# Similarity stage of a graph network: the owners' scans write PSUM in six runs, and each run is multiplied from there

## The chip, the cores and the metric

The kernel runs on one core of a Trainium2 chip. The metric is the device time of one launch in microseconds (us). Three runs of the kernel before took 16588.64, 16588.69 and 16592.46 us, median 16588.69.

## The reference

Four graph layers run over 12,500 nodes with 64 features each and 212,500 directed edges, sorted by `dst`. After each layer comes a residual sum and a layer norm. The changed stage is in the third layer:

```python
Wh = h @ W + b
row, col = (edge_index[0], edge_index[1])          # src, dst
dot = jnp.sum(Wh[row] * Wh[col], axis=-1)
nr, nc = norms of Wh[row] and Wh[col]
sim = dot / jnp.maximum(nr * nc, EPS)
base = adj_v * sc * no_diag
prop_pos = segment_sum((base * relu(sim))[:, None] * Wc, row)
prop_neg = segment_sum((base * -relu(-sim))[:, None] * Wc, row)
return scale * (coeff[0] * prop_pos + coeff[1] * prop_neg + coeff[2] * Wh)
```

## The kernel before

The kernel is a sequence of phases with a barrier between any two. Edges are padded to 128 x 1664: partition p holds 1664 consecutive edges, and an edge pass goes over them in 26 chunks of 64 edges per partition (NCH = 26, T = 64). The third layer's edges stand in the order of their row node (`src`), so the edges of one owner are neighbours.

`similarity_pass` (line 2270) is one such pass. For each chunk it needs two rows of 65 numbers for each edge, the 64 features of Wh and its norm:

- The other end's row is gathered. `gathers` (line 919) issues 64 indirect DMAs for a chunk from GpSimd (POOL), each of which fetches one row for each of 128 partitions from `tab65`, into `rows[b]`, one of two buffers. GpSimd may refill a buffer once the messages of the chunk that used it are made (semaphore `msg`), and once the chunk's indices are there.
- The owner's row is not gathered. An earlier phase wrote it into `spread` at the owner's first edge only, with zeros elsewhere. SyncE loads a chunk of it as `own` (line 2312), ScalarE turns it to feature-major order in `UB` (line 2351), 65 features of 65 places each, where place 0 carries the value from the chunk before. VectorE then spreads it over the owner's edges with a scan, state = mask * state + x (line 2401). `mask` lies in PSUM and is 0 at an owner's first edge, and at place 0 of each feature, so that one scan can run over several features.

In a chunk VectorE works in one written order: the first half of an unrelated side job (`dist.dve`, line 1046, the distance values of the fourth layer, 16 edges per partition of it beside each chunk); three scans over 22, 22 and 21 features, in place in `UB` (line 2401); the carry copy of place T to place 0 (line 2404); then, once the gathered rows have landed, the product `tmp = u * g` over 64 edges x 64 features (line 2416), its sum over features (line 2417), the product of the norms (line 2418) and seven small instructions that turn the two into a weight `a`; the message `MB = g * a` (line 2429); three scans that sum messages by owner (line 2434); a carry copy; and the second half of the side job. ScalarE copies the sums back to edge order in `tmp` (line 2363), and SyncE stores them (line 2319). ScalarE refills `UB` once the messages are made, and the mask once the message scans are done.

SyncE's order in a step is: wait until the chunk before's rows have landed (for the index buffer), load indices, base weights, `own` and the side job's input, then wait for ScalarE's copy and store it. `gains`, `ss` and `a` (two names in the tile `small`) lie in PSUM too.

Of the kernel before, what the change touches and what calls it, by code (L numbers as in the profile page):

```python
# [8 lines left out]
ALU = mybir.AluOpType  # L9
# [3 lines left out]
P = 128  # L13
F = 64
# [5 lines left out]
T = 64  # L20
# [13 lines left out]
def gnn_resnorm(nc, x_in, src_0, dst_0, attr3_0, attr64_0, attr64T_0, w_0, w2_0, W, out):  # L34
# [11 lines left out]
    def ps(ctx, name, shape, dt=F32):  # L46
        unique[0] += 1
        return ctx.enter_context(nc.psum_tensor(f"{name}_{unique[0]}", shape, dt))
# [3 lines left out]
    def sem(name):  # L52

        unique[0] += 1
        phase_sems.append(nc.alloc_semaphore(name=f"{name}_{unique[0]}"))
        return phase_sems[-1]
# [72 lines left out]
    DW = 16  # L129
# [2140 lines left out]
    def similarity_pass(last):  # L2270


        W_, TB, FM = F + 1, T + 1, 22
        runs = lambda w: [(f, min(f + FM, w)) for f in range(0, w, FM)]
        S = lambda n: [sem(f"L2_{n}{b}") for b in range(2)]
        q = lambda n: sem(f"L2_{n}")
        idx_in, rows_in, base_in_ = S("idx"), S("rows"), S("base")
# [3 lines left out]
        with ExitStack() as c, nc.Block() as block:  # L2281
            idx = [alloc(c, f"idx{b}", [P, T], I32) for b in range(2)]
            rows = [alloc(c, f"rows{b}", [P, T, W_]) for b in range(2)]
            own = alloc(c, "own", [P, T, W_])
            base = [alloc(c, f"base{b}", [P, T]) for b in range(2)]
            tmp = alloc(c, "tmp", [P, T, F])
            UB, MB = alloc(c, "UB", [P, W_, TB]), alloc(c, "MB", [P, F, TB])
            dot, nn, b2 = (alloc(c, f"s{n}", [P, T]) for n in range(3))
            mask, pa, gains = ps(c, "mask", [P, FM, TB]), ps(c, "pa", [P, P]), ps(c, "gains", [P, 4, F])
            small = ps(c, "small", [P, DW + T])  # L2290
            ss, a = small[:, 0:DW], small[:, DW:DW + T]
            UB_flat, MB_flat, mask_flat = (t.rearrange("p f t -> p (f t)") for t in (UB, MB, mask))
            by_edge = lambda t: t.rearrange("p f t -> p t f")
            dist = Distances(c, "L2", 3, 1, pa, gains, ss)

# [49 lines left out]
            def _(act):  # L2345
                def take(ch):
                    act.wait_ge(own_in, ch * 16 + 16)
                    if not (isinstance(ch, int) and ch == 0):
                        act.wait_ge(msg, ch)
                    act.wait_ge(own_kept, ch + 1)  # L2350
                    act.activation(UB[:, :, 1:TB], own.rearrange("p t f -> p f t"), ACT.Copy).then_inc(taken, 1)

                def flags(ch):
# [30 lines left out]
            def _(dve):  # L2384
# [2 lines left out]
                dve.memset(mask[:, :, 0:1], 0.0).then_inc(begun, 1)  # L2387
                dve.memset(last[:, :], 0.0).then_inc(begun, 1)
                dist.start(dve)
                NS = 10  # L2390

                def step(i, b):
                    ch = i * 2 + b
# [1 line left out]
                    dist.dve(dve, i, b, 0, 0)  # L2395
                    dve.wait_ge(taken, ch + 1)
                    dve.wait_ge(masked, ch + 1)
                    dve.wait_ge(own_kept, ch + 1)
                    for f0, f1 in runs(W_):
                        x = UB_flat[:, f0 * TB:f1 * TB]  # L2400
                        t = dve.tensor_tensor_scan(x, mask_flat[:, 0:(f1 - f0) * TB], x, 0.0, ALU.mult, ALU.add)
                    t.then_inc(filled, 1)
                    dve.wait_ge(filled, ch + 1)
                    dve.tensor_copy(UB[:, :, 0], UB[:, :, T]).then_inc(own_kept, 1)
                    u, g = by_edge(UB[:, :, 1:TB]), rows[b]
                    dve.wait_ge(rows_in[b], (i + 1) * 16 * T)
                    dve.wait_ge(base_in_[b], (i + 1) * 16)
                    if not first:
                        dve.wait_ge(stored, ch * 16)
                    n = [0]  # L2410

                    def link(ins):
                        n[0] += 1
                        ins.then_inc(steps, 1)
                        dve.wait_ge(steps, ch * NS + n[0])
                    link(dve.tensor_tensor(tmp[:, :, :], u[:, :, 0:F], g[:, :, 0:F], ALU.mult))
                    link(dve.reduce_sum(dot[:, :], tmp[:, :, :], axis=AX.X))
                    link(dve.tensor_tensor(nn[:, :], u[:, :, F], g[:, :, F], ALU.mult))
                    link(dve.tensor_scalar(nn[:, :], nn[:, :], 1e-8, None, ALU.max))
                    link(dve.reciprocal(a, nn[:, :]))  # L2420
                    link(dve.tensor_tensor(dot[:, :], dot[:, :], a, ALU.mult))
# [184 lines left out]
```

## Time and profile before

| | |
|---|---|
| median of 3 runs | 16588.69 us |
| the profiled execution | 16589.27 us, of which the span is 16587.6 us |
| busy over the span | GpSimd 72%, VectorE 60%, ScalarE 29%, TensorE 23% |
| VectorE's first and last product of line 2416 | start at 11935.95 and 14086.44 us |

A share of the span is an average over phases with different limits. The similarity pass lies between about 11855 and 14135 us, and what bounds it is read from that stretch alone.

### The profile page before, as it was taken

The numbers are of one execution on the slowest core, as the hardware profiler recorded it, in microseconds if no ns is written. First come the engines' busy times: TensorE is split into PE (matmuls) and PEld (weight loads), VectorE is DVE, ScalarE is ACT, GpSimd is POOL, SyncE is SP. The second block draws the span as 40 slices with busy tenths as digits, with TensorE's granted clock in tenths as the row PEclk, the third lists the DMA queues.
The fourth block names the chain that finished last, engine by engine and source line by source line (L and its number), as shares of the span: only waits on it lengthen the run. The fifth ranks groups of instructions, "written<-read, shape, count | busy, mean of one in ns | idle before, by whom it ended". The sixth has DMA issues, their size and how long they took to land. (4 is left out here: it accounts for less than half of the span.)

```text
span 16587.6 us, 97960 instructions
## 1 busy us (share of the span) xinstructions
PE 3852.7 (23%) x21926; PEld 2977.5 (18%) x21926; DVE 9987.8 (60%) x15135; ACT 4885.9 (29%) x4591; POOL 11956.4 (72%) x12292
## 2 busy tenths in 40 slices
PE   2333357777412111111111111111111111100000
PEld 1222246666401000000000111111100000100000
DVE  7777787777573333322222477777465555577877
ACT  1111112222102222223333244443133333244442
POOL 6777757777627777767777677776777777677776
PEclk7555578888755555555555555555555555555555
DMA  2222222222262222212222243443223222344443
GB/s 85 65 59 59 59 86 79 76 73 79 94 248 56 59 59 59 64 51 59 64 59 60 67 133 128 130 133 112 59 82 83 80 80 77 104 158 154 159 160 110
DMA packets 573888, 1516.80 MB, mean 91 GB/s; under 512 B 266952, under 2 KB 267485, under 8 KB 530066
## 3 DMA queue, kind: packets, MB, share of 16 engines
q1 hardware_dynamic: 179342, 1028.88, 16.9%
q0 software_dynamic: 392160, 467.91, 12.9%
q10 hardware_dynamic: 2068, 16.12, 0.2%
q8 instruction: 157, 2.57, 0.1%
q14 instruction: 161, 1.32, 0.0%
HBM read 714.46 MB, written 803.57 MB: 92 GB/s over the span
## 5 line engine op out<-in xcount | busy, mean ns | idle before, releaser
L927 POOL DMA_INDIRECT rows<-tab,idx x4992 | 4867.3, 975 | 1583.9 <-issue 1520.4
L574 POOL DMA_INDIRECT moved_rows<-recs,sidx x1664 | 1724.8, 1037 | 544.1 <-issue 506.9
L1812 POOL DMA_INDIRECT rows<-tab,idx x1664 | 1580.7, 950 | 535.2 <-issue 506.8
L927 POOL DMA_INDIRECT rows<-in_x,idx x1664 | 1588.1, 954 | 511.1 <-issue 506.8
L927 POOL DMA_INDIRECT rows<-sums,idx x1664 | 1570.0, 944 | 513.5 <-issue 506.8
L1410 DVE TENSOR_TENSOR_SCAN FB<-mask,FB 128x1430 f32<-128x1430 f32 x156 | 463.8, 3028 | 1835.0 <-ACT FB L1383 1835.0
L990 PE MATMUL dist_ps<-dist_w,a3T 65*128 65x512 f32 x416 | 392.8, 1100 | 4132.4 <-ACT a3T L1018 4106.6
L1057 DVE TENSOR_REDUCE small<-SQ 128x16 f32<-128x1024 f32 x156 | 191.1, 1225 | 1296.1 <-ACT SQ L1037 728.8
L990 PEld LDWEIGHTS dist_ps<-dist_w,a3T 65*128 65x128 f32 x416 | 122.2, 324 | 4273.1 <-issue 4060.4
L1383 ACT ACTIVATE FB<-rows 128x4096 f32<-128x4096 f32 x52 | 371.2, 7138 | 1345.6 <-DMA rows<-tab,idx 752.7
L1823 PE MATMUL lg<-bd_fcr,attrT 128*128 128x128 f32 x1664 | 339.9, 395 | 1726.7 <-DVE lx L1893 1715.0
L611 ACT ACTIVATE place<-pP 128x98 f32<-128x98 f32 x832 | 210.2, 253 | 1594.7 <-PE pP L765 1589.4
L1823 PEld LDWEIGHTS lg<-bd_fcr,attrT 128*128 128x128 f32 x1664 | 326.5, 305 | 1740.1 <-DVE lx L1893 1725.9
L747 PE MATMUL pE<-ohT 128*128 128x256 f32 x1664 | 617.3, 458 | 37.3 <-ACT ohT L601 37.2
L338 PE MATMUL H_d<-oh_dl,oh_dh 128*98 128x128 bf16 x1664 | 365.8, 313 | 750.7 <-DVE oh_sh L323 750.7
L1918 DVE TENSOR_TENSOR_SCAN PV<-lx,PV 128x1792 f32<-128x1792 f32 x128 | 490.9, 3877 | 73.6 <-ACT lx L1847 73.6
L1288 DVE TENSOR_TENSOR_SCAN rows<-held,last,rows 128x64 f32<-128x64 f32 (+1 forms) x1664 | 405.0, 326 | 208.3 <-DMA rows<-in_x,idx 208.3
L1854 ACT ACTIVATE DN<-PV 128x1664 f32<-128x1664 f32 x128 | 409.4, 3248 | 409.3 <-DVE PV L1918 409.3
L1065 DVE TENSOR_TENSOR Y<-Y,gains 128x1024 f32<-128x1024 f32 x416 | 507.6, 1220 | 14.2
L1952 PE MATMUL pT<-ident,lastmax 128*64 128x128 f32 x2 | 0.8, 393 | 2196.5 <-PEq L63 2196.5
L1730 DVE TENSOR_TENSOR_SCAN PV<-lx,PV 128x896 f32<-128x896 f32 x256 | 503.9, 2010 | 4.4
L658 DVE CUSTOM_DVE_ANT_0 junk<-pV,ohh 128x98 f32<-128x98 f32 x1664 | 428.4, 257 | 129.1 <-PE pV L763 96.5
(464 smaller groups left out, 18853.4 us busy)
## 6 DMA issues: line engine op xcount, KB each, us to landing
sums<-DN SPq DMA_DIRECT2D x128, 1664.0 KB, 6.6
rows<-tab,idx POOLq DMA_INDIRECT x6656
spread<-zeros SPq DMA_DIRECT2D x52, 1040.0 KB
own<-spread SPq DMA_DIRECT2D x26, 2080.0 KB
sums<-rows SPq DMA_DIRECT2D x26, 2048.0 KB, 6.6
dists<-Y SPq DMA_DIRECT2D x104, 512.0 KB, 2.7
recs<-sums SPq DMA_DIRECT2D x26, 2048.0 KB, 13.0
sums<-OUT SPq DMA_DIRECT2D x26, 2048.0 KB
```

The costliest lines, as they stand in the source:

```text
L574: pool.indirect_dma_start(moved_rows if fill else rec, bass.IndirectOffsetOnAxis(ap=idx[b][:, j:j + 1], axis=0), recs[b][:, j, :], None).t ...
L658: dve.tensor_tensor_reduce(out=junk[:, :], in0=pV[h][:, k, 0:HI], in1=ohh[b][:, t, :], scale=1.0, scalar=0.0, op0=ALU.mult, op1=ALU.add, a ...
L747: pe.matmul(pE[h][:, 0:2, :].rearrange("p a e -> p (a e)"), o[:, 2 * h, :], o[:, 2 * h:2 * h + 2, :].rearrange("p a e -> p (a e)"), start= ...
L927: pool.indirect_dma_start(rows[b][:, j, :], None, table, bass.IndirectOffsetOnAxis(ap=idx[b][:, j:j + 1], axis=0)).then_inc(rows_in[b], 16)
L990: t = pe.matmul(self.p1[:, 8 * h:8 * h + 8, :].rearrange("p a f -> p (a f)"), self.a3T[:, :], dist_w[:, h * 512:(h + 1) * 512], start=True ...
L1065: link(dve.tensor_tensor(Y[:, :, :], Y[:, :, :], v, op))
L1410: t = dve.tensor_tensor_scan(x, mask_flat[:, 0:(f1 - f0) * TB], x, 0.0, ALU.mult, ALU.add)
L1730: t = dve.tensor_tensor_scan(a, lx_flat[h], a, 0.0, ALU.mult, ALU.add)
L1812: pool.indirect_dma_start(rows[b][:, j, :], None, table, bass.IndirectOffsetOnAxis(ap=idx[b][:, j:j + 1], axis=0)).then_inc(rows_in[b], 16)
L1823: t = pe.matmul(lg[:, h, :], attr_T[b][:, h, :], bd["fcr"][:, :], start=True, stop=True)
L1854: act.activation(DN[:, :, s_ * F:(s_ + 1) * F], by_edge(PV[:, s_, :, 1:TL + 1]), ACT.Copy).then_inc(copied, 1)
L1918: t = dve.tensor_tensor_scan(a, lx_flat, a, 0.0, ALU.mult, ALU.add)
```

## The change

Three scans in place in `UB` become six scans over 11 features (the last over 10), which read `UB` and write a new PSUM tile `whole`. Behind each scan stand a small carry copy from `whole` to `UB`, and the product of that run's features with the gathered rows, read from `whole`. All of these now stand behind the wait for the gathered rows, for the base weights and for the store of `tmp`. `FM` is also the run length of the message scans, which become six as well (11, 11, 11, 11, 11 and 9 features). The mask tile shrinks from 22 to 11 features, and `gains`, `ss` and `a` move into one PSUM tile.

```diff
-        W_, TB, FM = F + 1, T + 1, 22
+        W_, TB, FM = F + 1, T + 1, 11
         runs = lambda w: [(f, min(f + FM, w)) for f in range(0, w, FM)]
+        NR = len(runs(W_))
...
-            mask, pa, gains = ps(c, "mask", [P, FM, TB]), ps(c, "pa", [P, P]), ps(c, "gains", [P, 4, F])
-            small = ps(c, "small", [P, DW + T])
-            ss, a = small[:, 0:DW], small[:, DW:DW + T]
+            mask, whole, pa = ps(c, "mask", [P, FM, TB]), ps(c, "whole", [P, FM, TB]), ps(c, "pa", [P, P])
+            various = ps(c, "various", [P, 4 * F + DW + T])
+            gains = various[:, 0:4 * F].rearrange("p (n f) -> p n f", f=F)
+            ss, a = various[:, 4 * F:4 * F + DW], various[:, 4 * F + DW:4 * F + DW + T]
...
-                    act.wait_ge(own_kept, ch + 1)
+                    act.wait_ge(own_kept, ch * NR + 1)
...
-                NS = 10
+                NS = 2 * NR + 8
...
                     dve.wait_ge(masked, ch + 1)
-                    dve.wait_ge(own_kept, ch + 1)
-                    for f0, f1 in runs(W_):
-                        x = UB_flat[:, f0 * TB:f1 * TB]
-                        t = dve.tensor_tensor_scan(x, mask_flat[:, 0:(f1 - f0) * TB], x, 0.0, ALU.mult, ALU.add)
-                    t.then_inc(filled, 1)
-                    dve.wait_ge(filled, ch + 1)
-                    dve.tensor_copy(UB[:, :, 0], UB[:, :, T]).then_inc(own_kept, 1)
-                    u, g = by_edge(UB[:, :, 1:TB]), rows[b]
+                    dve.wait_ge(own_kept, ch * NR + 1)
                     dve.wait_ge(rows_in[b], (i + 1) * 16 * T)
                     dve.wait_ge(base_in_[b], (i + 1) * 16)
                     if not first:
                         dve.wait_ge(stored, ch * 16)
+                    g = rows[b]
...
-                    link(dve.tensor_tensor(tmp[:, :, :], u[:, :, 0:F], g[:, :, 0:F], ALU.mult))
+                    for f0, f1 in runs(W_):
+                        w = (f1 - f0) * TB
+                        link(dve.tensor_tensor_scan(whole_flat[:, 0:w], mask_flat[:, 0:w], UB_flat[:, f0 * TB:f1 * TB], 0.0,
+                                                    ALU.mult, ALU.add))
+                        dve.tensor_copy(UB[:, f0:f1, 0], whole[:, 0:f1 - f0, T]).then_inc(own_kept, 1)
+                        if f1 > F:
+                            dve.tensor_tensor(nn[:, :], whole[:, F - f0, 1:TB], g[:, :, F], ALU.mult).then_inc(filled, 1)
+                        last_f = min(f1, F)
+                        link(dve.tensor_tensor(tmp[:, :, f0:last_f], by_edge(whole[:, 0:last_f - f0, 1:TB]), g[:, :, f0:last_f], ALU.mult))
                     link(dve.reduce_sum(dot[:, :], tmp[:, :, :], axis=AX.X))
-                    link(dve.tensor_tensor(nn[:, :], u[:, :, F], g[:, :, F], ALU.mult))
+                    dve.wait_ge(filled, ch + 1)
```

`link` lets VectorE wait for the instruction just issued.

## Rows read from the trace of the kernel before

**Rows 1.** Groups by line and shape, 11855:14150 us: busy, mean ns, idle before, releaser.

```profile
L927 POOL DMA_INDIRECT rows<-tab,idx x1664 | 1723.2, 1036 | 518.5 <-issue 506.8 <-DMA idx<-sdst 11.7
L2416 DVE TENSOR_TENSOR tmp<-UB,rows 128x4096 f32<-128x4096 f32 x26 | 193.7, 7450 | 488.8 <-DMA rows<-tab,idx 488.8
L2429 DVE TENSOR_TENSOR MB<-rows,small 128x4096 f32<-128x4096 f32 x26 | 192.8, 7417 | 0.9
...
L2418 DVE TENSOR_TENSOR s<-UB,rows 128x64 f32<-128x64 f32 x26 | 7.1, 271 | 0.9
```

**Rows 2.** GpSimd in order of time: start, us, instruction; one chunk boundary.

```profile
12968.03 0.94 POOL L927 DMA_INDIRECT rows<-tab,idx  x1 [0.30 <-issue]
12969.28 7.06 POOL L927 DMA_INDIRECT rows<-tab,idx  x1 [0.30 <-issue]
```

**Rows 3.** VectorE in order of time, one chunk and the boundary of rows 2.

```profile
12882.08 7.46 DVE L2416 TENSOR_TENSOR tmp<-UB,rows 128x4096 f32<-128x4096 f32 x1 [17.81 <-DMA rows<-tab,idx]
...
12941.01 9.05 DVE L2401 TENSOR_TENSOR_SCAN UB<-mask,UB 128x1430 f32<-128x1430 f32 x3 [0.33 <-DVE Y L1065]
12968.12 7.45 DVE L2416 TENSOR_TENSOR tmp<-UB,rows 128x4096 f32<-128x4096 f32 x1 [17.80 <-DMA rows<-tab,idx]
...
12982.64 7.42 DVE L2429 TENSOR_TENSOR MB<-rows,small 128x4096 f32<-128x4096 f32 x1
```

**Rows 4.** Another phase, 5013:7100 us: GpSimd's group, and VectorE's product of that shape.

```profile
L927 POOL DMA_INDIRECT rows<-tab,idx x1664 | 1570.1, 944 | 532.1 <-issue 506.8 <-DMA idx<-src_d 25.3
...
L1419 DVE TENSOR_TENSOR OUT<-FB,small 128x4096 f32<-128x4096 f32 x26 | 193.6, 7448 | 0.0
```

**Rows 5.** Start of the stage in order of time: SyncE, ScalarE and GpSimd.

```profile
11853.43 0.43 SPq L2312 DMA_DIRECT2D own<-spread  x1
...
11861.46 7.79 ACT L2351 ACTIVATE UB<-own 128x4160 f32<-128x4160 f32 x1 [52.69 <-DMA own<-spread]
...
11857.32 0.95 POOL L927 DMA_INDIRECT rows<-tab,idx  x1 [0.30 <-issue]
```

**Rows 6.** SyncE at the boundary of rows 2, and the store's time to landing.

```profile
12969.19 0.33 SPq L2312 DMA_DIRECT2D own<-spread  x1
...
13008.09 0.36 SPq L2319 DMA_DIRECT2D sums_s<-tmp  x1
...
sums_s<-tmp SPq DMA_DIRECT2D x26, 2048.0 KB, 6.9
```

**Rows 7.** VectorE's groups by line and shape, of the whole trace or this pass.

```profile
L1706 DVE TENSOR_TENSOR_SCAN Hp<-lx,Hp,kx 128x896 f32<-128x896 f32 x128 | 266.2, 2080 | 12.1 <-DVE lx L1698 12.0
L1698 DVE TENSOR_TENSOR lx<-side,rows 128x416 f32<-128x416 f32 x256 | 153.8, 601 | 395.2 <-DMA rows<-tab,idx 388.6
L1893 DVE COPY lx<-lg 128x1664 f32<-128x1664 f32 x64 | 117.6, 1838 | 8.2 <-PE lg L1823 8.2
L1913 DVE TENSOR_TENSOR PV<-PV 128x864 f32<-128x864 f32 x128 | 135.5, 1059 | 233.7 <-ACT PV L1844 231.5
L2417 DVE TENSOR_REDUCE s<-tmp 128x64 f32<-128x4096 f32 x26 | 114.9, 4420 | 0.9
L2437 DVE COPY MB<-MB 128x64 f32<-128x64 f32 x26 | 5.8, 224 | 0.9
...
L1996 DVE COPY cin<-pB 128x64 f32<-128x64 f32 x1 | 0.2, 224 | 0.5 <-PE pB L1956 0.5
```

**Rows 8.** First product; then the stage's end: last gather, last product, last store.

```profile
11935.95 7.45 DVE L2416 TENSOR_TENSOR tmp<-UB,rows 128x4096 f32<-128x4096 f32 x1 [43.85 <-DMA rows<-tab,idx]
...
14083.93 0.94 POOL L927 DMA_INDIRECT rows<-tab,idx  x1 [0.30 <-issue]
...
14086.44 7.44 DVE L2416 TENSOR_TENSOR tmp<-UB,rows 128x4096 f32<-128x4096 f32 x1 [17.75 <-DMA rows<-tab,idx]
...
14131.53 0.33 SPq L980 DMA_DIRECT2D dists<-Y  x1
```

**Rows 9.** Phase of line 1913, whole trace: its gathers' group on GpSimd.

```profile
L1812 POOL DMA_INDIRECT rows<-tab,idx x1664 | 1580.7, 950 | 535.2 <-issue 506.8 <-ACT idx L1834 28.4
```

More of the change, by code:

```diff
@@ L2288, in similarity_pass @@
             dot, nn, b2 = (alloc(c, f"s{n}", [P, T]) for n in range(3))
-            mask, pa, gains = ps(c, "mask", [P, FM, TB]), ps(c, "pa", [P, P]), ps(c, "gains", [P, 4, F])
-            small = ps(c, "small", [P, DW + T])
-            ss, a = small[:, 0:DW], small[:, DW:DW + T]
-            UB_flat, MB_flat, mask_flat = (t.rearrange("p f t -> p (f t)") for t in (UB, MB, mask))
+            mask, whole, pa = ps(c, "mask", [P, FM, TB]), ps(c, "whole", [P, FM, TB]), ps(c, "pa", [P, P])
+            various = ps(c, "various", [P, 4 * F + DW + T])
+            gains = various[:, 0:4 * F].rearrange("p (n f) -> p n f", f=F)
+            ss, a = various[:, 4 * F:4 * F + DW], various[:, 4 * F + DW:4 * F + DW + T]
+            UB_flat, MB_flat, mask_flat, whole_flat = (t.rearrange("p f t -> p (f t)") for t in (UB, MB, mask, whole))
             by_edge = lambda t: t.rearrange("p f t -> p t f")
```

## The prediction

> **What bounds the kernel now.** The page gives averages over all phases, so I went from it to the groups of instructions by line in the stretch of this pass, then to the order of time around one chunk boundary. GpSimd issues 1664 gathers there, 26 chunks of 64, and but for 11.7 us at the start its idle time is all "issue", some 0.30 us in front of each gather [rows 1]. It never waits for a buffer or an index once it runs. So the gather stream sets the pace, and VectorE waits for it: 17.80 us in front of one product, 488.8 us over 26 [rows 1, 3]. A chunk takes 86.0 us: (14086.44 - 11935.95) / 25, the first and the last product of line 2416 [rows 8].
>
> The gathers do not all take the same time. Most take 0.94 us, 1.25 us with the idle time, but one in a chunk takes 7.06 us [rows 2]. It begins at 12969.28, 1.16 us after VectorE began its product at 12968.12, and ends at 12976.34, 0.77 us after the product ended at 12975.57 [rows 2, 3]. 64 x 1.25 = 80 us, and the long one adds 6.1: that is the 86.0. Over the stage the gathers' mean is 1036 ns. In an earlier phase, also 1664 gathers beside the same side job, it is 944 ns [rows 1, 4]. The difference in busy time, 1723.2 - 1570.1 = 153.1 us, is 25 x 6.12: one long gather for each product except the last, behind which no gather runs [rows 8].
>
> **Which work makes it long.** The product reads two SBUF operands, `UB` and `rows`. Line 2429 has the same shape and length (7.42 us) but takes its second operand from PSUM (`small`), and line 1419 in the other phase is alike: 7448 ns, one operand in PSUM, gathers at 944 ns beside it [rows 1, 4]. Nor do the scans of line 2401 (9.05 us, mask in PSUM) or the sum of line 2417 (4.42 us, one input) have a long gather beside them. What is left is VectorE with two SBUF inputs, for longer than about 1.3 us (7.45 less the 6.12 that is lost). A DMA is the other suspect, since SyncE issues the 2 MB load of `own` at 12969.19 [rows 6]. But at the start of the stage the same load is issued at 11853.43 and has landed by 11861.46, and the gathers in that time keep 0.94 to 0.96 us [rows 5].
>
> **What the change removes.** After it the large products read `whole` from PSUM and only `rows` from SBUF, the form of line 2429. The long gather should go, in 25 chunks: -153 us, and the chunk falls from 86.0 to 79.9 us.
>
> **What it adds to VectorE.** Everything below stands between the landing of the rows and the message, one chunk at a time.
> - Six scans, each waited for: five of 715 elements, one of 650. The old three take 9.05 us for 4225 elements, 2.14 ns each, with hardly a fixed cost, as they are not waited for one by one [rows 3]; that is the lower end. A scan that is waited for takes 2080 ns for 896 elements, 0.16 above that rate [rows 7]. From it, 1.69 and 1.55 us, together 10.0.
> - Six products, five of 704 elements, one of 576. The source in PSUM is stepped through by 65 words for each element. In SBUF such steps cost 1.82 ns an element (7450 / 4096) against 1.08 without (4420 / 4096, line 2417) [rows 1, 7]. No row reads PSUM in steps with all else in runs, but two write it so at full rate: line 1893, 1664 elements in 1838 ns, and line 1698, 416 in 601 [rows 7]. I go by the latter, as it is nearest in kind: 0.60 + 288 x 1.04 ns = 0.90 us, and 0.77 for the last, together 5.3 us. The upper end is 7.45 plus six fixed costs of 0.17, 8.5 us.
> - Six carry copies of 11 elements. A copy out of PSUM of 64 takes 0.224 us [rows 7]; 0.17 each without 53 elements, 1.0 us, and from below nothing where they lie in the shadow of the neighbours.
> - The norms' product, 0.27 us [rows 1], moved; 12 handovers of 0.04 us (0.9 us idle over 26, line 2429 [rows 1]), 0.5 us.
>
> Sum 17.1 us. It replaces 7.45 + 0.27 + 0.08 = 7.8. The message scans become six, three fixed costs more, between 0 and the 0.16 above; I take 0.1 each, +0.3 us. So each chunk's chain behind the landing grows by **9.6 us**. With all lower ends (scans 9.05, copies and extra scans nothing) it is 7.0, with all upper ones (products 8.5, copies 0.22 each, extra scans 0.5) 13.3; I keep 7 to 14.
>
> Two rules of the Trainium skill weigh against this. Its page "Vector Engine (DVE) Microarchitecture Reference" (5.2, Measured stream behaviour) says that an SBUF port drops to about 1.7 to 1.8 ns an element where each element hops; line 2416 agrees with 1.82, but the rule is given for SBUF, and no row here shows a stepped read of PSUM. If it held there too, the products would keep their 7.45 us and the end would come some 3 us later. The page "VectorE: DVE Perf Modes" (the TRN2 errata) gives instructions that read PSUM 62 cycles more fixed cost than those that read SBUF, an estimate of 0.8 us over 12 of them; line 1996 copies 64 elements out of PSUM in 0.224 us, and line 2437 as many within SBUF in the same time, so the trace does not bear it out [rows 7].
>
> **What hides it.** Before, the three scans lay in VectorE's idle time ahead of the landing, at no cost. Now they stand behind it, and the cover is what is left of the chunk. From one landing to the next side-job half's end VectorE needed 12941.01 - 12882.08 = 58.9 us (product to the next chunk's first scan [rows 3]); with 9.6 that is 68.5, under 79.9. So 11 us of idle time stay, 7 at the upper bound. GpSimd needs `msg` of two chunks back, made 22 us behind the landing before (12982.64 + 7.42 [rows 3]) and 31 now: far ahead. SyncE issued the store of `tmp` 40.0 us behind the landing (13008.09 - 12968.12), and it takes 6.9 [rows 6]; now 49.6 + 6.9 = 56.5 us, ahead of the wait for `stored` that has moved in front of the scans. Base weights and `own` are loaded right behind the landing before. ScalarE's refill of `UB`, the mask, and the copy back each move by 9.6 within the chunk, and nothing waits at SyncE behind them except the next index load, which needs the next landing. The index load of the chunk after next stays right behind the landing and has a whole chunk in hand.
>
> **What shows.** Only in the last chunk nothing covers the chain: everything from the last product at 14086.44 to the side job's store at 14131.53 and the barrier behind it [rows 8] moves by 9.6 us. The first landing at 11936 [rows 8] doesn't move; the scans of chunk 0 simply wait for it.
>
> Sum on the profiled execution: span 16587.6 - 153.0 + 9.6 = 16444.2; 1.7 us lie around it (16589.27 - 16587.6), so 16445.9. The runs' median stands 0.6 below the profiled one: **16445.3 us**, 0.86% faster.
>
> **The rivals.**
> 1. *Pieces of the stall remain.* If a product from PSUM still hindered GpSimd, six pieces of 0.9 us a chunk would do so. The nearest row is line 1913: 128 products of two SBUF inputs, 1.06 us each, in a phase whose gathers take 950 ns instead of 944 [rows 7, 9], so 1664 x 6 ns = 10 us, 0.08 each. 150 pieces x 0.08 = 12 us: 16457. At 0.4 us each it would be 60: 16505. Against it: line 2429 leaves no trace at all on the gathers.
> 2. *The stall is not the product's inputs.* Something else at the landing holds the gather (a load of SyncE, the wake of VectorE). Then 6.1 us a chunk stay and only the tail grows: 16588.7 + 9.6 = 16598, no change by the measure below. For it: all these events fall within 1.2 us. Against it: the undisturbed gathers beside the first load of `own` [rows 5], and the stall that ends with the product.
> 3. *VectorE becomes the bound*, the slower side. The place is the new block of scans and products behind the landing, if PSUM serves stepped reads or two streams of one engine much worse than SBUF. The gather pace is lost from 79.9 - 58.9 = 21 us of added chain on, and the gain is gone from 27 us on, when the chunk is 86 again. With products at 6.5 ns an element (26.6 us instead of 5.3) the chain grows by 30.9, the chunk is 89.8, and 25 x 3.8 + 31 = 126 us are lost: 16715. Against it: writes to PSUM in such steps run at 1.1 ns [rows 7].
>
> **How the numbers follow.** Forecast 88%, rival 1 5% (mostly its small form), rival 2 4%, rival 3 3%. Differences under 0.2%, 33 us, count as no change, about what a measurement of this kernel tells apart. Rival 1 in both forms is faster, so faster 93%, same 4%, slower 3%. The chain's bounds, 7 to 14, give 16443 to 16450; the stall's 147 to 154 us and a few us between runs (16588.64 to 16592.46 before) widen it, and the small form of rival 1 reaches 16457: range 16438 to 16464.
>
> **What would show it.** In the profile after, the gathers of this stage should have a mean of 944 ns and none above 1.2 us; the scans' line should start at the landing, 79.9 us apart; VectorE's idle time in front of it should be about 11 us and be ended by the gathers' DMA; the six scans and products should take some 17 us to the sum of line 2417's kind. I am wrong if a long gather stands beside a product or a scan, if GpSimd waits for `msg` or an index load, or if the wait in front of the scans ends with `taken` or `stored`. Only the size is off if the products cost 1.3 us each.

## The result, and the profile after

The changed kernel took 16459.72 us (median of 16484.86, 16442.27, 16438.67 and 16477.18), beside 16588.67 us for the kernel before on the same chip (median of 16588.64, 16588.69, 16592.46 and 16587.58). The ratio is 0.9914 [0.9899, 0.9928]: faster, by 129 us at the medians. The forecast was 16445.3, within 7 us of the two lower runs and 32 to 40 us under the two upper ones. The lower runs are what the prediction's own terms give; what lifts the upper one that was profiled lies in another phase, shown below.

The profiled execution is the uppermost one: 16484.86 us, span 16483.2 us (before 16589.27 and 16587.6), so 104.4 us of the span are gone. Measured from the start of the first to the end of the last gather of each phase, the difference splits up like this:

| stretch | before | after | difference |
|---|---|---|---|
| similarity pass, first to last gather | 2230.1 | 2076.8 | -153.3 |
| its end, last gather to the first gather of line 2127 | 59.5 | 67.9 | +8.4 |
| attention pass (line 1812) | 2087.5 | 2117.8 | +30.3 |
| sort (line 574) | 2231.7 | 2238.4 | +6.7 |
| the rest | | | about +3.5 |

The groups by line and shape in the similarity pass after, 11855:14050 us (count, then busy us and mean ns, then idle before and its releaser):

```profile
L927 POOL DMA_INDIRECT rows<-tab,idx x1664 | 1570.0, 944 | 518.4 <-issue 506.8 <-DMA idx<-sdst 11.6
L2414 DVE TENSOR_TENSOR_SCAN whole<-mask,UB 128x715 f32<-128x715 f32 x130 | 215.0, 1654 | 394.3 <-DMA rows<-tab,idx 390.7
L2438 DVE TENSOR_TENSOR_SCAN MB<-mask,MB 128x715 f32<-128x715 f32 x130 | 202.7, 1626 | 0.9
L2433 DVE TENSOR_TENSOR MB<-rows,various 128x4096 f32<-128x4096 f32 x26 | 192.8, 7416 | 0.9
...
L2420 DVE TENSOR_TENSOR tmp<-whole,rows 128x704 f32<-128x704 f32 x130 | 114.4, 880 | 0.0
L2414 DVE TENSOR_TENSOR_SCAN whole<-mask,UB 128x650 f32<-128x650 f32 x26 | 39.5, 1519 | 0.9
L2416 DVE COPY UB<-whole 128x11 f32<-128x11 f32 x130 | 23.2, 178 | 4.5
L2420 DVE TENSOR_TENSOR tmp<-whole,rows 128x576 f32<-128x576 f32 x26 | 19.5, 751 | 0.0
```

Against [rows 1] the gathers' mean falls from 1036 to 944 ns, to the nanosecond that of the phase in [rows 4], and GpSimd still waits for no buffer. The 153.1 us of busy time that were set against one long gather a chunk are gone. The wait of VectorE for the landing is now in front of the scans, and still 390.7 us in sum: the gathers set the pace as before, only sooner.

VectorE after, in order of time, one chunk (start, us):

```profile
12933.07 1.66 DVE L2414 TENSOR_TENSOR_SCAN whole<-mask,UB 128x715 f32<-128x715 f32 x1 [13.38 <-DMA rows<-tab,idx]
12934.76 0.18 DVE L2416 COPY UB<-whole 128x11 f32<-128x11 f32 x1
12934.84 0.88 DVE L2420 TENSOR_TENSOR tmp<-whole,rows 128x704 f32<-128x704 f32 x1
12935.76 1.65 DVE L2414 TENSOR_TENSOR_SCAN whole<-mask,UB 128x715 f32<-128x715 f32 x1
...
12949.11 4.42 DVE L2421 TENSOR_REDUCE s<-tmp 128x64 f32<-128x4096 f32 x1
...
12955.95 7.41 DVE L2433 TENSOR_TENSOR MB<-rows,various 128x4096 f32<-128x4096 f32 x1
12963.40 9.06 DVE L2438 TENSOR_TENSOR_SCAN MB<-mask,MB 128x715 f32<-128x715 f32 x6
```

The copy lasts 0.18 us, but the product behind it starts 0.08 us after the copy did: they overlap. The block from the landing to the sum takes 12949.11 - 12933.07 = 16.04 us, and the idle time in front of it is 13.38 us. In [rows 3] the product started on the landing with 17.80 us of idle time in front.

What the gain is lessened by in this execution sits in the attention pass, which the change does not touch. Before, GpSimd and VectorE in order of time beside one product of line 1913:

```profile
9628.25 0.95 POOL L1812 DMA_INDIRECT rows<-tab,idx  x1 [0.30 <-issue]
9629.50 1.23 POOL L1812 DMA_INDIRECT rows<-tab,idx  x1 [0.30 <-issue]
...
9628.85 2.15 DVE L1913 TENSOR_TENSOR PV<-PV 128x864 f32<-128x864 f32 x2 [3.58 <-ACT PV L1844]
```

And after:

```profile
9636.34 0.95 POOL L1812 DMA_INDIRECT rows<-tab,idx  x1 [0.30 <-issue]
9637.59 1.65 POOL L1812 DMA_INDIRECT rows<-tab,idx  x1 [0.30 <-issue]
9639.54 0.94 POOL L1812 DMA_INDIRECT rows<-tab,idx  x1 [0.30 <-issue]
...
9637.36 2.15 DVE L1913 TENSOR_TENSOR PV<-PV 128x864 f32<-128x864 f32 x2 [3.57 <-ACT PV L1844]
```

Both operands of that product lie in SBUF. How late a gather gets depends on where within the product it starts: before, only 21 gathers of this pass are above 1150 ns and the excess over 944 ns beside the product sums to 8.7 us; after, 63 are, with 40.9 us. That difference, 32 us, accounts for the pass's +30.3. Taken from VectorE's first product of line 1913 in one chunk to that in the next, the steps of this pass alternate between some 35.3 and 29.9 us in the execution before, and in the one after nearly all take 33.1. These two patterns are called rhythms below. The change isn't needed for the second one: the profiled run of `six_pieces_sbuf`, described below, whose attention pass is that of the kernel before, has the steps of 33.1 us, 63 late gathers and a pass of 2118.3 us, while its sort takes 2231.3 us as before. Without the pass and the sort's 6.7 us the changed kernel would stand at 16448, beside its lower runs of 16438.7 and 16442.3.

The experiments met two surroundings that neither kernel controls, a first in which the kernel before takes about 16,600 us and a second in which it takes 20,773 to 20,866 us (medians), and totals are compared only within one of them.

### The profile page after: what moved, and what is told of

Read it like the earlier page. It is cut to its first block and busy times, and to the rows that moved or that the text cites. A ratio compares the mean times of both kernels' runs of the same rounds, so it can differ in the third digit from the quotient of the medians.

```text
span 16483.2 us, 98678 instructions
## 1 busy us (share of the span) xinstructions
PE 3824.8 (23%) x21926; PEld 2959.1 (18%) x21926; DVE 9957.1 (60%) x15551; ACT 4870.5 (30%) x4591; POOL 11842.2 (72%) x12292
## 5 line engine op out<-in xcount | busy, mean ns | idle before, releaser
L927 POOL DMA_INDIRECT rows<-tab,idx x4992 | 4716.2, 945 | 1583.3 <-issue 1520.4
L574 POOL DMA_INDIRECT moved_rows<-recs,sidx x1664 | 1731.5, 1041 | 544.9 <-issue 507.0
L1812 POOL DMA_INDIRECT rows<-tab,idx x1664 | 1611.0, 968 | 535.3 <-issue 506.8
L1057 DVE TENSOR_REDUCE small<-SQ 128x16 f32<-128x1024 f32 x104 | 127.4, 1225 | 1082.6 <-ACT SQ L1037 724.9
L1854 ACT ACTIVATE DN<-PV 128x1664 f32<-128x1664 f32 x128 | 408.7, 3243 | 409.3 <-DVE PV L1918 409.3
L1664 ACT ACTIVATE DN<-PV 128x1664 f32<-128x1664 f32 x128 | 404.5, 3208 | 335.5 <-DVE PV L1730 335.5
```

What stands on the lines that cost most here:

```text
L574: pool.indirect_dma_start(moved_rows if fill else rec, bass.IndirectOffsetOnAxis(ap=idx[b][:, j:j + 1], axis=0), recs[b][:, j, :], None).t ...
L927: pool.indirect_dma_start(rows[b][:, j, :], None, table, bass.IndirectOffsetOnAxis(ap=idx[b][:, j:j + 1], axis=0)).then_inc(rows_in[b], 16)
L1812: pool.indirect_dma_start(rows[b][:, j, :], None, table, bass.IndirectOffsetOnAxis(ap=idx[b][:, j:j + 1], axis=0)).then_inc(rows_in[b], 16)
L1854: act.activation(DN[:, :, s_ * F:(s_ + 1) * F], by_edge(PV[:, s_, :, 1:TL + 1]), ACT.Copy).then_inc(copied, 1)
```

## The experiments

Theory: a gather that starts while VectorE runs a product with two SBUF inputs ends only behind that product, and this alone was the 153 us. Rivals: cutting the product is what helps, PSUM or not; the operand in PSUM is incidental and the order behind the landing does it; the rest belongs to the load of `own`.

### The changed kernel again

No edit.

> The changed kernel once more, unaltered. Its four times lay at 16439, 16442, 16477 and 16485 us, those of before within 5 us. The profiled one (16484.9) has its extra 40 us outside the changed pass: 30 us in the untouched attention pass (gathers of line 1812, 2117.8 us against 2087.5), 7 in the untouched edge sort. Theory A, chance: the attention pass settles in one of two rhythms at each execution, in either kernel. Then the new times fall in two groups near 16440 and 16480, and with as many runs of before some of those lie 30 us above 16588 too. Theory B, the change itself upsets that pass (code placement): then the changed kernel keeps its spread and before stays within 5 us. In both, the gathers of the similarity pass take 2076.8 us from first to last.

Measured, median of 11 runs: 20853.33 us beside 20835.46, ratio 1.0005 [0.9996, 1.0014], in the second surroundings. Neither the gain nor a loss was there, and the two groups of times that the expectation asks about can't be read there either. Another chip gave the same:

> The changed kernel unaltered, on another chip, since on the first its gathers were paced by something else. Theory A (two rhythms of the attention pass, by chance and in either kernel): the kernel before, in the last measurement at 16598 once and at 16620 to 16629 six times, already shows two groups; the changed kernel shows two as well, about 143 us lower each, and the ratio is 0.9914. In the profile the attention pass takes 2087 or 2118 us, the similarity pass 2077. Theory B (the change upsets the attention pass): the changed kernel has more of the slow group than before has on this chip.

20874.94 us (median of 10 runs) beside 20866.05, ratio 1.0007 [0.9992, 1.0023]. GpSimd in this run, in order of time:

```profile
16540.57 1.09 POOL L927 DMA_INDIRECT rows<-tab,idx  x1 [0.30 <-issue]
16541.97 1.10 POOL L927 DMA_INDIRECT rows<-tab,idx  x1 [0.30 <-issue]
16543.37 1.11 POOL L927 DMA_INDIRECT rows<-tab,idx  x1 [0.30 <-issue]
```

Here gathers follow each other by 1.40 us instead of the 1.25 of [rows 2], with nothing in the chain but their own "issue"; over the pass the mean is 1.38 us. The similarity pass takes 2303.6 us. What paces the gathers at 1.40 us was not found. What the runs do show is that the pass then takes 2303 to 2310 us in every variant, so that what a product does to one gather cannot be read from the total there. It can be read in two other places. One is the single gather. The other is the start of the pass: the slow pace isn't there yet. In this run the first two chunks of gathers take 80.1 and 80.0 us, as in the first surroundings, the third takes 82.5, and only from the fourth on do they take some 88 to 90. The next three experiments are read in these two ways.

### One operand of the small products back in SBUF

```diff
-            mask, whole, pa = ps(c, "mask", [P, FM, TB]), ps(c, "whole", [P, FM, TB]), ps(c, "pa", [P, P])
+            mask, whole, pa = ps(c, "mask", [P, FM, TB]), alloc(c, "whole", [P, FM, TB]), ps(c, "pa", [P, P])
```

> The changed kernel with the tile `whole` in SBUF instead of PSUM: the same six scans and products, but each product (704 elements) has two SBUF inputs. Theory 1, it is the two SBUF inputs, and a gather that starts within such a product ends 0.8 us after it: the gathers hindered are those that start less than the product's rest before its end, between 0 and 0.75 us more each, by where the product falls in the 1.25 us period; some 0.2 us on the mean, so 1 to 2 us a chunk, 25 to 50 us in the pass (2076.8 becomes 2100 to 2130 us). If strided SBUF reads also slow the products to 1.3 us each, up to 3 us a chunk, 2150. Rival, the stall of before came with the landing (SyncE's loads or a single long instruction) and has gone with the splitting alone: 2077 us as with PSUM.

Measured: 20850.54 us (second surroundings), so the total tells nothing. The groups of line 2420 and of the gathers in this run's pass:

```profile
L2420 DVE TENSOR_TENSOR tmp<-whole,rows 128x704 f32<-128x704 f32 x126 | 179.6, 1425 | 0.0
...
L927 POOL DMA_INDIRECT rows<-tab,idx x1664 | 1774.7, 1067 | 541.3 <-issue 529.7 <-DMA idx<-sdst 11.6
```

With the source in SBUF 112 gathers beside line 2420 take over 1.5 us, with a median of 1.66 us and 81 us of excess over 944 ns in all; with the source in PSUM, in `same_again`, there were 3. Taken from 1.15 us on, each of the 150 products that have gathers beside them has its late one, with 99.5 us of excess, against 22 gathers and 8.2 us. The second chunk takes 84.0 us, against 80.0. So the price is about 4 us a chunk, above the 1 to 3 us expected: between two of these products stands a scan of 1.65 us, and each product finds a new gather. Order, number of instructions and bytes are those of the changed kernel, so the place of the tile `whole` makes the difference. It also prices the steps: the same product takes 1425 ns from SBUF and 880 ns from PSUM.

### The message product given two SBUF inputs

```diff
-            various = ps(c, "various", [P, 4 * F + DW + T])
+            various, a_sb = ps(c, "various", [P, 4 * F + DW + T]), alloc(c, "a_sb", [P, T])
-            ss, a = various[:, 4 * F:4 * F + DW], various[:, 4 * F + DW:4 * F + DW + T]
+            ss, a = various[:, 4 * F:4 * F + DW], a_sb[:, :]
```

> The changed kernel with the weight `a` in SBUF instead of PSUM, so that the message product of 7.42 us (g * a) gets two SBUF inputs; nothing else is altered. Theory 1 (two SBUF inputs hold the gathers back for the length of the product): one long gather of 7.0 us appears again in each chunk, now beside the message product, some 26 us behind the landing: chunk 79.9 to 86.0, pass 2077 to 2230 us, total +150 us. Rival (the stall belongs to the landing): no long gather, 2077 us.

All three runs of it (the labels with _2 and _3 are the same kernel) met the second surroundings: 20842.63, 20887.27 and 20848.03 us. This is the sharpest test of the cause, as line 2433 is far from the landing and from SyncE's loads. GpSimd of the third run in order of time, then VectorE:

```profile
17009.46 0.95 POOL L927 DMA_INDIRECT rows<-tab,idx  x1 [0.86 <-issue]
17010.72 8.00 POOL L927 DMA_INDIRECT rows<-tab,idx  x1 [0.30 <-issue]
17019.02 0.94 POOL L927 DMA_INDIRECT rows<-tab,idx  x1 [0.30 <-issue]
...
17010.60 7.43 DVE L2433 TENSOR_TENSOR MB<-rows,a_sb 128x4096 f32<-128x4096 f32 x1
```

The gather starts 0.12 us within the product and ends at 17018.72, 0.69 us after the product's end at 17018.03. In each of the three runs there are 25 such gathers, with medians of 7.42 to 7.43 us and 163.0 to 165.6 us of excess. An operand of 64 weights per partition, moved from PSUM to SBUF, makes the stall appear where it never was. The rival that ties it to the landing or to the load of `own` falls.

> The changed kernel with the weight `a` in SBUF, once more, to read its price in time. On the first chip it had 25 long gathers of 7.43 us beside the message product, but another limit hid their price. Theory 1: the similarity pass takes 2230 us instead of 2077, the total is 150 us above the changed kernel on this chip. Rival, long gathers are made good later by a queue of work behind them: 2077 us in spite of them.

> The changed kernel with the weight `a` in SBUF, a third time, for its price on a chip where the gathers pace the pass (two earlier times it met the other kind of chip: 25 long gathers, no price). Theory 1: similarity pass 2230 us instead of 2077, one gather of about 7.0 us beside each message product. Rival, made good later: 2077 us.

The price in the total, expected at +150 us in the first surroundings, was not to be had: the pass took 2308 to 2310 us, 5 to 7 more than the changed kernel's. The start of the pass has it. The first two message products of `weight_in_sbuf_3`:

```profile
15837.66 7.42 DVE L2433 TENSOR_TENSOR MB<-rows,a_sb 128x4096 f32<-128x4096 f32 x1
15924.09 7.42 DVE L2433 TENSOR_TENSOR MB<-rows,a_sb 128x4096 f32<-128x4096 f32 x1
```

They lie 86.43 us apart (86.36 and 86.37 in the other two runs), where those of `same_third` lie 80.05 apart: 6.3 to 6.4 us for one long gather, and four chunks in a row show it, before the slow pace sets in. From then on a chunk takes 88 to 91 us with a long gather or without. The gaps from one gather's start to the next show how. Of 1663 gaps, `weight_in_sbuf_3` has 1341 under 1.3 us and 25 over 3 us; the changed kernel (`same_third`) has 806 under 1.3 and 665 between 1.3 and 1.5. Behind every long gather but the last at least 36 come at under 1.3 us and make it good. What limits the gathers there is not shown.

### The kernel before with its second operand in PSUM

```diff
-                    link(dve.tensor_tensor(tmp[:, :, :], u[:, :, 0:F], g[:, :, 0:F], ALU.mult))
+                    link(dve.tensor_tensor(tmp[:, :, :], u[:, :, 0:F], gains[:, 0, :].unsqueeze(1).to_broadcast([P, T, F]), ALU.mult))
```

This kernel multiplies by a vector in PSUM instead of the gathered rows; the similarity isn't computed.

> The kernel before, with one operand of its large product changed from the gathered rows (SBUF) to a row of `gains` (PSUM), read once for each edge; so the similarity is not computed, and all else, the waits, the landing, SyncE's loads and the order, stays. Theory 1: the long gather goes, pass 2230 to 2077 us, and as the scans keep their place ahead of the landing the tail doesn't grow: 16589 - 153 = 16436 us. Rival (the stall belongs to the landing or to SyncE's loads): the long gather of 7.06 us stays, 2230 us, 16589 us.

> The kernel before with the gathered rows replaced by a row of `gains` (PSUM) in the large product, so that the similarity is not computed; once more, for its price in time. Theory 1: pass 2077 us instead of 2230, tail as before (59.5 us from the last gather to the next phase's first one, 67.9 in the changed kernel), total 153 us below before on this chip. Rival (the landing or SyncE's loads hold the gather): 2230 us.

> The kernel before with a row of `gains` (PSUM) in place of the gathered rows in the large product, so that the similarity is not computed, a third time, for the same reason. Theory 1: pass 2077 us instead of 2230, last gather to the next phase's first one 59.5 us as before. Rival (landing or SyncE's loads): 2230 us.

Again three times the second surroundings: 20815.02, 20852.25 and 20856.75 us, the pass 2303 to 2305 us. The product's group in the third run, and its gathers in short (shortest, median and longest ns):

```profile
L2416 DVE TENSOR_TENSOR tmp<-UB,gains 128x4096 f32<-128x4096 f32 x25 | 186.4, 7457 | 62.9 <-DMA rows<-tab,idx 62.4
...
L927 POOL DMA_INDIRECT rows<-tab,idx x1664: 940/952/1938, 15747.7 to 18051.6; - x185
```

The product has its old length (7457 ns against 7450 in [rows 1]), its old place behind the landing and its old shape, and the longest gather is 1.94 us instead of 7.06. The kernel before was not traced in these surroundings, but the three runs above show that a stall of 7.4 us occurs in them. So neither the length nor the place makes the stall. Together with the three runs above this settles the cause. The first two products of this run, and below them the second of the kernel before, whose first starts at 11935.95 [rows 8]:

```profile
15828.89 7.47 DVE L2416 TENSOR_TENSOR tmp<-UB,gains 128x4096 f32<-128x4096 f32 x1 [43.92 <-DMA rows<-tab,idx]
15908.81 7.46 DVE L2416 TENSOR_TENSOR tmp<-UB,gains 128x4096 f32<-128x4096 f32 x1 [12.04 <-DMA rows<-tab,idx]
...
12021.90 7.45 DVE L2416 TENSOR_TENSOR tmp<-UB,rows 128x4096 f32<-128x4096 f32 x1 [18.03 <-DMA rows<-tab,idx]
```

They lie 79.92 us apart (79.80 and 79.78 in the other two runs) instead of 85.95: with the product uncut, the operand's place alone gives back the 6 us of a chunk. Over the whole pass, in the first surroundings, this edit stays unmeasured.

### The cut alone, both inputs in SBUF

```diff
-                NS = 10
+                NS = 15
...
-                    link(dve.tensor_tensor(tmp[:, :, :], u[:, :, 0:F], g[:, :, 0:F], ALU.mult))
+                    for f in range(0, F, 11):
+                        link(dve.tensor_tensor(tmp[:, :, f:min(f + 11, F)], u[:, :, f:min(f + 11, F)], g[:, :, f:min(f + 11, F)], ALU.mult))
```

> The kernel before, with its large product cut into six linked products over 11 features (the last over 9), all else as it was: both inputs in SBUF, scans ahead of the landing, no tile `whole`. Each piece takes about 1.3 us. Theory 1 as it stands after the first runs: a gather that starts within a product of two SBUF inputs ends about 0.8 us behind that product, and the next starts 0.3 us later, so it meets the rest of the next piece (0.2 us) and ends hardly late. So cutting alone should give back most of the stall: first gather up to 0.9 us late, the others some 0.05 to 0.2, in sum 1 to 2 us a chunk instead of 6.1; pass 2230 becomes 2100 to 2130 us on a chip like that of the first measurement, total 16460 to 16490. Rival, 'PSUM is what counts': the pieces follow each other with a gap of 0.04 us, GpSimd finds no room in it, and the stall stays at about 6 us a chunk: 2230 us, 16589. On the chip of the runs before this one (before at 20835) another limit sets the gather pace of this pass (2303 us in every variant), and neither would show in the total; there the gathers beside the pieces tell: single ones of up to 1.8 us, or one of 7.

Measured, in the first surroundings, median of four runs: 16500.7 us beside 16623.57, ratio 0.9923 [0.9906, 0.9939]; the pass takes 2106.5 us, within the 2100 to 2130 expected. In the kernel before, with nothing moved to PSUM, the cut alone brings 123.6 of the 153.3 us, so the first rival named above holds in good part: cutting helps, PSUM or not. VectorE's pieces, then GpSimd beside them, in order of time:

```profile
12943.12 8.69 DVE L2417 TENSOR_TENSOR tmp<-UB,rows 128x704 f32<-128x704 f32 x6 [11.55 <-DMA rows<-tab,idx]
...
12944.33 1.02 POOL L927 DMA_INDIRECT rows<-tab,idx  x1 [0.30 <-issue]
...
12950.13 1.19 POOL L927 DMA_INDIRECT rows<-tab,idx  x1 [0.31 <-issue]
```

Between two pieces lie 0.04 us, and that is enough for one gather to get through: it ends 0.76 us behind the end of the piece in which it started, well within the next one. The gathers fall into step with the pieces: one for each piece, some 1.50 us apart instead of 1.25, until the block is over. That costs 29.7 us over the pass (2106.5 against 2076.8), 1.2 us a chunk, where the uncut product costs 6.1. Taking the operand from PSUM as well is worth these remaining 30 us.

### The same cut in the attention pass

The changed kernel with the product of line 1913 in eight pieces of 216 elements instead of two of 864.

```diff
-                    for h in range(2):
-                        e = slice(h * F // 2, (h + 1) * F // 2)
+                    for h in range(8):
+                        e = slice(h * F // 8, (h + 1) * F // 8)
...
-                        dve.wait_ge(weighed, ch * 2 + h + 1)
+                        dve.wait_ge(weighed, ch * 8 + h + 1)
```

> The changed kernel with the attention pass's product of lines 1910 to 1914 (two SBUF inputs, two pieces of 864 elements, 1.06 us) cut into eight pieces of 216 elements, some 0.39 us each. By the rule read from the traces (a gather that starts within such a product ends 0.8 us behind it, where it would take 0.94) a piece can make a gather late by at most its length less 0.13 us: 0.93 us with two pieces, 0.25 with eight. Theory A: the attention pass then takes 2077 to 2085 us in every execution, the two groups of times merge, and the kernel lies at or below the lower group of the changed kernel, 10 to 40 us below its median. Six more instructions cost VectorE some 1.3 us a chunk of 26 gathers, which it has (3.5 us of waiting for the gathers per chunk). Rival (the two groups come from elsewhere, or the added instructions make VectorE the bound of that pass, nearly balanced as it is): two groups stay, or the pass takes over 2120 us.

Second surroundings, median of four runs: 20676.03 us beside 20866.05, ratio 0.9908 [0.9891, 0.9924]. The attention pass fell from 2636.0 us (`same_third`) to 2441.3, far from the 2077 to 2085 expected, which were for the first surroundings. Its gathers here:

```profile
L1812 POOL DMA_INDIRECT rows<-tab,idx x1664 | 1576.6, 947 | 893.1 <-issue 497.4 <-ACT idx L1834 395.7
```

and in the changed kernel in the same surroundings:

```profile
L1812 POOL DMA_INDIRECT rows<-tab,idx x1664 | 1617.3, 972 | 1046.7 <-ACT idx L1834 544.2 <-issue 502.6
```

The gathers' busy time falls by 40.7 us, as the mechanism has it. Most of the rest, 148.5 us, are waits for ScalarE's copy of the indices. They are much larger in these surroundings (28 us in the first), and why they shrink with the cut was not settled.

### A version that beats both

The changed kernel, the eight pieces, and one more product with two SBUF inputs moved to PSUM: the one-hot comparison of the sort phase (line 642, in this kernel 644), whose iota row gets a copy in PSUM.

```diff
+                link(dve.tensor_copy(iota_p, iota[:, :].bitcast(F32)))
...
-                        u = iota[:, 0:w].unsqueeze(1).to_broadcast([P, 4, w])
+                        u = iota_p.bitcast(BF16)[:, 0:w].unsqueeze(1).to_broadcast([P, 4, w])
```

> The changed kernel with two more edits of the same kind in untouched phases: the attention pass's product in eight pieces (as in attention_eight), and in the edge sort the row of numbers that the one-hot comparisons of line 642 read in PSUM instead of SBUF (they had two SBUF inputs, 686 and 560 ns, two in a row, 832 in all). Theory 1 (two SBUF inputs hold gathers and scatters back): in the sort the 249 long scatters beside line 642 (109.8 us in the changed kernel's profile, 7 more beside line 650) go, the phase takes 2085 to 2130 us instead of 2231 to 2238, unless the chain of TensorE, ScalarE and VectorE behind it binds first; attention pass 2077 to 2087; similarity pass 2077. On a chip where before takes 16590 to 16625: 16300 to 16350 us, ratio 0.982 to 0.985, and the times lie within 10 us. Rival (the sort's stalls are its own chain's, or VectorE reads slower from PSUM and binds): sort still 2200 us or more, ratio 0.989 to 0.991. On a chip like that of the last runs (before at 20866), where gathers and other instructions come at another pace, the similarity pass gains nothing, the attention pass some 190 us as in attention_eight, and the sort little: ratio 0.990.

Measured, first surroundings, median of six runs: 16322.24 us beside 16617.9, ratio 0.982 [0.9785, 0.9854]. The groups of this run:

```profile
L575 POOL DMA_INDIRECT moved_rows<-recs,sidx x1664 | 1611.5, 968 | 545.8 <-issue 506.2 <-DVE sidx L691 39.6
...
L1814 POOL DMA_INDIRECT rows<-tab,idx x1664 | 1572.0, 945 | 534.5 <-issue 506.9 <-ACT idx L1836 27.6
...
L644 DVE TENSOR_TENSOR ohl<-lo,spare 128x512 bf16<-128x512 bf16 x416 | 283.7, 682 | 0.0
L1915 DVE TENSOR_TENSOR PV<-PV 128x216 f32<-128x216 f32 x512 | 196.9, 384 | 246.9 <-ACT PV L1846 231.3
```

The profile of the changed kernel has these two gather groups at means of 1041 and 968 ns:

```profile
L574 POOL DMA_INDIRECT moved_rows<-recs,sidx x1664 | 1731.5, 1041 | 544.9 <-issue 507.0
L1812 POOL DMA_INDIRECT rows<-tab,idx x1664 | 1611.0, 968 | 535.3 <-issue 506.8
```

The sort takes 2118.4 us (2238.4 after), the attention pass 2078.9 (2117.8), the similarity pass 2077.0. With the two edits the 30 us between two groups of runs are gone as well: the six runs lie between 16316.8 and 16325.2, while the kernel before on that chip has one group at 16583 to 16593 and one at 16611 to 16621, with one run of 16782 apart. So the kernel before has two groups too. That they are the rhythms of the attention pass is the likeliest reading: between the profiles of before and `six_pieces_sbuf` that pass differs by 30.8 us and the sort by 0.4. But the sort's edit went with the attention pass's here, so no run tells the two edits' effect on the groups apart. Within the lower group the changed kernel gains 148 us (16588.7 to 16440.5, the mean of its two lower runs), close to the 143 forecast.

## Why the prediction was right, point by point

- **The bound.** Right. The gathers of GpSimd pace the pass before and after; GpSimd waits for no message and for an index only at the start (11.6 us in both).
- **What makes the gather long.** Right: two SBUF inputs, shown by putting the second input in PSUM with all else kept, and by making the stall appear at the message product. The sum for it, -153.0, measured -153.3. One clause was wrong: "for longer than about 1.3 us" is no limit, as the products of 1.06 us in the attention pass and those of 0.69 and 0.56 us in the sort hinder gathers too. By the Trainium skill, "GPSIMD Engine Reference" (8. Key points), GpSimd shares its SBUF interfaces with VectorE, with contention where a VectorE instruction has two SBUF inputs; the runs agree. That page gives no size; the 7.06 us gather beside a 7.45 us product is this case's.
- **The stepped read of PSUM.** The prediction took 1.04 ns an element from line 1698 and was right: 704 elements in 880 and 576 in 751 ns differ by 1.01 ns an element. In SBUF a further element cost more: 1.86 ns in `six_pieces_sbuf` (1461 ns for 704, 1223 for 576) and 1.99 in `whole_in_sbuf` (1425 and 1170). The rule weighed against this, from the Trainium skill's "Vector Engine (DVE) Microarchitecture Reference" (5.2, Measured stream behaviour), gives an SBUF port 1.7 to 1.8 ns where each element hops. These rows lie somewhat above it in SBUF, and in PSUM there is no such penalty.
- **The chain behind the landing.** 17.1 us were worked out, 16.04 measured. Scans 5 x 1.654 + 1.519 = 9.8 (10.0 expected), products 5 x 0.880 + 0.751 = 5.15 (5.3). The copies were priced at 1.0 us and cost about 0.5, as each is covered but for 0.08 us. The message scans take 9.06 us against 8.92 before, where 0.3 was added. So the chain grew by some 8.4 us instead of 9.6, within the bounds; the text's lower bound of 7 is 7.3 by its own terms. The second rule weighed, from the Trainium skill's "VectorE: DVE Perf Modes" (the TRN2 errata), gives reads of PSUM 62 cycles more fixed cost than reads of SBUF. It is not borne out either: 64 elements took 224 ns from either [rows 7], and 11 elements out of PSUM take 178 ns.
- **What hides it.** Right: the chain shows only in the last chunk, +8.4 us. VectorE's idle time is 13.4 us, not the 11 forecast: with the shorter chain 79.9 - 58.9 - 8.4 = 12.6 us would be left, and where the other 0.8 come from is not shown. The last landing to the side job's last store took 14025.08 - 13971.59 = 53.5 us, against 45.1 [rows 8]. The wait for `stored` never comes last; its store is issued 12980.95 - 12933.07 = 47.9 us behind the landing (49.6 expected) and has landed well within the chunk.
- **The rivals.** None held. Pieces of the stall do not remain: no gather of the pass is above 0.97 us. Rival 2 falls with `before_psum_operand`, which keeps the landing and the loads and loses the stall. Rival 1 is what happens where the pieces stay in SBUF, at 1.2 us a chunk, between its small form (0.5) and its large one (2.4). Rival 3 was as far off as its rows said.
- **What the sum left out.** It took every other phase as fixed. The attention pass is not: its product of two SBUF inputs and its gathers met in two rhythms in the two profiles, 30 us apart. That the four runs of the kernel before all lay in the lower group, and that those of the changed kernel fell two and two, was luck: with a third upper run the median would have been 16477 us or more, above the range. The prediction used it only to price rival 1, at 6 ns a gather [rows 7, 9], and those rows are of the favourable rhythm. The range, up to 16464, therefore was too narrow above: two of four runs lie over it, at 16477 and 16485. The reading was right and the spread was mis-sized.

What stays open: what sets the gathers' pace of 1.40 us in the second surroundings, where the change gives nothing in the total; what decides which rhythm the attention pass takes; and the gain over the whole pass of moving the uncut product's operand to PSUM in the first surroundings.

The last gather and the end of the stage after, GpSimd and SyncE, for the two ends used above:

```profile
13969.04 0.94 POOL L927 DMA_INDIRECT rows<-tab,idx  x1 [0.31 <-issue]
...
14025.08 0.33 SPq L980 DMA_DIRECT2D dists<-Y  x1
```

## What to carry to other kernels

Where GpSimd's DMAs set the pace, compare their mean duration between phases: a mean of 1036 beside 944 ns hid one gather of 7 us in each chunk, and what VectorE runs at that moment, not the chain of waits, shows the cause. Look for VectorE instructions that read two SBUF tensors; put one input into PSUM, or, if it doesn't fit, cut the instruction into pieces, which alone brought four fifths. A phase with short such instructions in a repeating order took one of two rhythms here from run to run, and a forecast should leave room for it. Where the total hides an effect, look at the start of the phase: there the price of one long gather, 6.3 to 6.4 us a chunk, stood plainly in surroundings in which the pass as a whole grew by 5 to 7 us.

## What was not expected of the hardware

- A gather already under way when the product starts keeps its 0.95 us; one that starts within it ends about 0.8 us behind the product's end (0.77 in the similarity pass before, 0.82 at the 63 late gathers of the attention pass after, 0.69 at the message product). Three that start within the first 24 ns of a product are not hindered. A gap of 0.04 us between two products lets one gather through.
- Short bf16 products count too: the sort's pairs of 0.69 and 0.56 us, 416 of each, cost that phase 113 us in the kernel before and 120 in the changed one (2231.7 and 2238.4 us against 2118.4), until one input lay in PSUM.
- Reading PSUM in steps of 65 words costs 1.01 ns for each further element, as little as line 1893 pays for its copy from PSUM to PSUM, stepped where it writes (1.10 ns, [rows 7]); SBUF in the same steps takes 1425 ns for the 704 elements that take 880 from PSUM.
- The same kernel on the same chip was seen with gathers 1.25 us apart (before: 16618 us) and, a few minutes later, 1.40 us apart over long stretches (before: 20773 us). In the latter stalls of 6.5 to 6.6 us a chunk add only 5 to 7 us to a pass of 2303 us, though the first of them, before the slow pace sets in, add 6.3 to 6.4 us each.
